# Selector and region products of layer one as 32x128 tiles instead of pairs of 32x64 tiles

## The reference, cut to what matters

```python
x = x + _L0_conv_ref(_gn(x), ...)      # shifted windows of 8x8 pixels, 16 heads of 16 channels
x = x + _L1_conv_ref(_gn(x), ...)      # causal and anti-causal attention over the whole image
```

```python
q = (xw @ Wq.T).reshape(-1, N, HEADS, d).transpose(0, 2, 1, 3)   # N = 64 tokens of a window, d = 16
k = (xw @ Wk.T).reshape(-1, N, HEADS, d).transpose(0, 2, 1, 3)
v = (xw @ Wv.T + bv).reshape(-1, N, HEADS, d).transpose(0, 2, 1, 3)
qn = q / jnp.maximum(jnp.linalg.norm(q, axis=-1, keepdims=True), 1e-12)
kn = k / jnp.maximum(jnp.linalg.norm(k, axis=-1, keepdims=True), 1e-12)
logits = jnp.einsum('bhnd,bhmd->bhnm', qn, kn) * scale
logits = logits + 16.0 * jax.nn.sigmoid(bias)
lg = jnp.where(mask[None, :, None], -jnp.inf, lg)                # mask: pixels of different regions
scores = jax.nn.softmax(logits, axis=-1)
o = jnp.einsum('bhnm,bhmd->bhnd', scores, v)
z = o @ Wo.T + bo
```

## Time and profile before

| | |
|---|---|
| median of 3 runs | 1212.93 us (1212.18 to 1214.43) |
| the profiled execution | 1214.44 us, its span 1212.7 us |
| TensorE busy | 1127.4 us, 93% |
| weight loads busy | 837.4 us, 69% |
| VectorE busy | 930.5 us, 77% |
| ScalarE busy | 640.7 us, 53% |
| one exponential of layer one (L621), mean | 1021 ns |
| mean granted TensorE clock | 0.969 of 2.4 GHz |

### The profile page before, as it was taken

The page is one execution under the profiler, slowest core; times in us unless marked ns, Lnnn a source line. Parts: engine busy times, 40 slices in busy tenths (PEclk is TensorE's granted clock), DMA queues, the critical chain, the costliest instruction groups (busy, mean ns, idle before and its releaser), DMA issues.

```text
span 1212.7 us, 50934 instructions
## 1 busy us (share of the span) xinstructions
PE 1127.4 (93%) x21342; PEld 837.4 (69%) x21342; DVE 930.5 (77%) x1669; ACT 640.7 (53%) x1051; POOL 199.9 (16%) x271
## 2 busy tenths in 40 slices
PE   6989998899799899979899999999999999999994
PEld 3767776777677677767667777777777777777762
DVE  4588888788788688864688788787878788787873
ACT  3465666566466456542545555555555555555550
POOL 1001111111011111111212221221222221221220
PEclk9799999899899899998999999999999999999997
DMA  2111111111111110000022222312222221312223
GB/s 85 49 37 40 42 42 29 39 37 38 40 37 37 41 38 23 24 23 11 10 55 46 63 54 51 70 39 67 44 62 44 61 56 49 70 40 65 44 65 78
DMA packets 189177, 55.93 MB, mean 46 GB/s; under 512 B 151172, under 2 KB 184214, under 8 KB 189078
## 3 DMA queue, kind: packets, MB, share of 16 engines
q1 hardware_dynamic: 184800, 53.06, 18.3%
q10 hardware_dynamic: 4280, 1.40, 0.5%
HBM read 35.95 MB, written 18.35 MB: 45 GB/s over the span
## 4 chain that ended last, share of the span: by engine, by line
PE 72%; DVE 15%; issue 7%; ACT 2%; DMA 2%; SPq 1%; DVEq 1%; ACTq 0%
PE psG L1103 13%; PE psA L500 10%; PE psA L1145 7%; PE psG L1125 5%; PE psE L1203 5%; PE psA L1164 5%; PE psA L1178 4%; PE psE L454 3%; DVE probs L736 3%; PE psA L488 3%; PE psA L440 3%; DVE stack L1430 3%; DVE stack L1425 3%; PE psE L475 2%; PE psG L396 2%
## 5 line engine op out<-in xcount | busy, mean ns | idle before, releaser
L1399 DVE TENSOR_REDUCE cm<-psG 128x4 f32<-128x1024 f32 (+1 forms) x192 | 234.9, 1224 | 117.0 <-PE psG L1125 116.9
L1261 ACT ACTIVATE probs<-psG 128x1024 f32<-128x1024 f32 x192 | 196.4, 1024 | 128.1 <-PE psG L1103 127.7
L1103 PE MATMUL psG<-stack 32*128 32x256 f32 (+1 forms) x2048 | 218.3, 341 | 7.1 <-DVE cm L1399 6.5
L1112 PE MATMUL psG<-stack 32*128 32x256 f32 (+1 forms) x2048 | 220.2, 342 | 1.7 <-DVE cm L1399 1.7
L1478 POOL TENSOR_SCALAR_AFFINE_SELECT probs<-probs 128x1024 f32<-128x1024 f32 x128 | 139.6, 1103 | 471.6 <-ACT probs L1261 471.5
L1103 PEld LDWEIGHTS psG<-stack 32*128 32x128 f32 x2048 | 149.8, 185 | 64.2 <-DVE cm L1399 27.6
L1112 PEld LDWEIGHTS psG<-stack 32*128 32x128 f32 x2048 | 149.9, 185 | 3.4 <-DVE cm L1399 1.9
L886 POOL TENSOR_TENSOR X<-X,probs 128x96 f32 (+5 forms) x128 | 55.0, 461 | 513.0 <-ACT probs L628 513.0
L500 PE MATMUL psA<-probs,xh 128*128 128x512 f32 x256 | 129.7, 633 | 2.1 <-ACT xh L661 1.4
L1164 PE MATMUL psA<-xh,wqk 128*128 128x256 f32 x512 | 121.5, 381 | 0.0
L1425 DVE RECIPROCAL stack<-stack 128x128 f32<-128x128 f32 x128 | 115.7, 929 | 4.0 <-DMA stack<-totals 4.0
(11 more groups left out here) (140 smaller groups left out, 1803.7 us busy)
## 6 DMA issues: line engine op xcount, KB each, us to landing
X<-in_xr SPq DMA_DIRECT2D x32, 256.0 KB, 3.7
probs<-inverses SPq DMA_DIRECT2D x32, 256.0 KB
stack<-scratch_heads SPq DMA_DIRECT2D x32, 256.0 KB
stack<-totals SPq DMA_DIRECT2D x64, 128.0 KB
out<-X SPq DMA_DIRECT2D x32, 256.0 KB, 3.0
scratch_heads<-stack SPq DMA_DIRECT2D x126, 64.0 KB
totals<-stack SPq DMA_DIRECT2D x126, 4.0 KB
inverses<-rd SPq DMA_DIRECT2D x32, 32.0 KB, 1.5
```

What stands on the lines that cost most here:

```text
L1103: last = nc.tensor.matmul(G[:, to:to + b.size], km[i.k][own_rows(r), o, e, b.keys_of(o) * P:(b.keys_of(o) + 1) * P], qm[i.k][own_rows(r), ...
L1112: nc.tensor.matmul(G[:, to:to + b.size], qm[j.k][own_rows(r), o, e, b.queries_of(o) * P:(b.queries_of(o) + 1) * P], km[j.k][own_rows(r), o ...
L1261: nc.scalar.activation(weights[i.k][:, b.weights_at:b.weights_at + 1024], G[:, base:base + 1024], ACT.Exp).then_inc(exp_done, 1)
L1399: nc.vector.reduce_max(slots, scores, AX_X).then_inc(max_done, 1)
```

## The change

In both places two products, one for each half of the output's partitions, become one product over all 128. The constants already lie side by side in SBUF (`pick` for e = 0 and 1, `region_queries` for the two windows), so no data moves. Each of the two stages now issues 8 products instead of 16 for an image, with the same 256 moving elements. The signals stay four for each stage. Everything else, the transpose of the maxima into the sums' bank included, is as it was.

```diff
@@ scores
                 for o in range(CT):
-                    for e in range(2):
-                        for r in range(QUADS):
-                            at = r * 512 + o * TOKENS
-                            last = nc.tensor.matmul(G[e * WTOK:(e + 1) * WTOK, at:at + TOKENS], pick[own_rows(r), 2 * o + e, :],
-                                                    ct[own_rows(r), :], start=False, stop=True,
-                                                    tile_position=(r * COL, e * WTOK), skip_group_check=True)
-                            if o == CT - 1 and e == 1:
-                                last.then_inc(s_ready, 1)
+                    for r in range(QUADS):
+                        at = r * 512 + o * TOKENS
+                        last = nc.tensor.matmul(G[:, at:at + TOKENS],
+                                                pick[own_rows(r), 2 * o:2 * o + 2, :].rearrange("p e k -> p (e k)"),
+                                                ct[own_rows(r), :], start=False, stop=True,
+                                                tile_position=(r * COL, 0), skip_group_check=True)
+                        if o == CT - 1:
+                            last.then_inc(s_ready, 1)
@@ bounds
                 for t in range(TT):
-                    for ww in range(2):
-                        for r in range(QUADS):
-                            at = r * 512 + t * TOKENS
-                            last = nc.tensor.matmul(G[ww * WTOK:(ww + 1) * WTOK, at:at + TOKENS],
-                                                    region_queries[own_rows(r), win(2 * t + ww)], region_keys[own_rows(r), :, :],
-                                                    start=False, stop=True, tile_position=(r * COL, ww * WTOK),
-                                                    skip_group_check=True)
-                            if t == TT - 1 and ww == 1:
-                                last.then_inc(max_ready, 1)
+                    for r in range(QUADS):
+                        at = r * 512 + t * TOKENS
+                        last = nc.tensor.matmul(G[:, at:at + TOKENS], region_queries[own_rows(r), t * P:(t + 1) * P],
+                                                region_keys[own_rows(r), :, :], start=False, stop=True,
+                                                tile_position=(r * COL, 0), skip_group_check=True)
+                        if t == TT - 1:
+                            last.then_inc(max_ready, 1)
```

## The result

| | before | after |
|---|---|---|
| median | 1213.12 us (1212.18 to 1214.43, 4 runs) | 1236.51 us (1233.68 to 1249.0, 4 runs) |
| ratio after to before | | 1.0212, 95% interval 1.0142 to 1.0282 |
| span of the profiled execution | 1212.7 us | 1233.7 us |
| TensorE busy, matmul records | 1127.4 us, 21342 | 1141.3 us, 20830 |

The change made the kernel slower by 23 us. The forecast, 4 us slower, had the sign and a sixth of the size, and the range ended at 1220.5.

What follows compares the result with a forecast made beforehand. VectorE was taken to pace 15 steps and a late TensorE 17, one of them hidden; 16 steps by 0.25 us gave 4.0 us, corrections cancelling, on 1212.93: 1216.9 us. Own range 1215 to 1219, wider range 1211.5 to 1220.5.

Steps and rivals of the forecast that it cites:

- The circle and the margin: VectorE's L736 to TensorE's L488, L500 and back takes 14.45 us; TensorE's margin before L488 is 0.69 or 0.30 us.
- The stop: Going from 32x64 to 32x128 tiles drains TensorE: 0.15 us before the selectors, 0.20 us before the region products.
- The slow load: Rival: 128 columns of a 32-row tile load slowly, 8.3 us more, 1221.2 us; chance 0.15 shared with a new issue wait.
- What hides it: The margin before L488 covers the added 0.25 us, so the 15 steps paced by VectorE cost nothing.
- The sum: Added TensorE time over 16 steps, 4.0 us; low clock, at most 0.75 more, and 0.9 less issue waiting cancel.
- the instructions arrive sooner: Rival: at L396 in three loop steps, shorter code removes issue waits, 7.8 us against the 4.0, 1209.1 us; chance 0.07.
- its converse: A new issue wait at a place like L396, 1219 to 1221 us; chance 0.15 shared with slowly loading weights.
- It must just happen to reach over that point: Condition for losing an issue wait at L396: a 4% instruction saving must reach the place where code is missing.
- The 16 steps by 0.25 us: Steps where TensorE is late, each paying 0.13 us at the selectors and 0.12 at the region products: 4.0 us.
- the hidden case: Rival: TensorE's added delay vanishes in later waits for issue, time near 1214 us; chance 0.20.
- the no-stop case: Rival: TensorE does not drain between 32x64 and 32x128 tiles, 1.9 us less, 1211.0 us; chance 0.08.

Runs made afterwards that it cites:

- the pair with equal code: Kernel before with 192 idle instructions at the start, 1203.49 us, and the same with 32x128 tiles and each product cut in two, 1204.58 us.
- the estimate above: Kernel before with 192 idle instructions at the start, less its 12.2 us of later start: would be at 1191 us, not run.

## Why the prediction was wrong

- *The circle and the margin*: right. The short rounds are 29.5 us before and after, and the margin shrank by the stops. In the pair with equal code the wait before the weighing went from 0.62 to 0.47 us and from 0.22 to none, where 0.37 and none were worked out.
- *The stop*: right, 0.15 and 0.20 us, the rounds 0.11 to 0.12 apart. From the last product of the stage ahead to the last one of the changed stage it is now 0.28 and 0.33 us in the raw starts (188.730 to 189.008 and 192.415 to 192.745), where 0.29 and 0.34 were worked out. The slow load did not come: it would have made them 0.39 and 0.44 us.
- *What hides it*: right for the steps in which VectorE sets the pace, as the equal short rounds show.
- *The sum*: this is the step that failed, "if the waits for issue, 15.3 + 8.3 = 23.6 us, shrink with them, 0.9 us is given back". I took the waits for issue to be a rate, so much waiting for so many instructions, and let them shrink by the 4% of instructions that go. Those of L396 in the loop come from rounds in which the loop is loaded again, each 6 to 7 us longer than a short one, and their number went from 3 to 7. The term was -0.9 us and measured +25.7 us in the loop. The trace of the kernel before already tells it, nine instruction packets in one round and none in the next; I had stayed with the waits.
- *The rivals*: "the instructions arrive sooner" named the place and had the wrong side; its converse, one new wait in some place, I priced at 2 to 4 us and not at four rounds. "It must just happen to reach over that point" was the right thought: either half of the change brings the loop to a place where it stays resident, and the whole change moves it on to one where it reaches further into an eighth block than before.
- *The 16 steps by 0.25 us*, 4.0 us: not confirmed. The pair with equal code shows 1.1 us between medians, inside the noise, and outside the loop the shorter code of the changed kernel is 4.7 us faster, not slower. What of that the stops took and what the code's new place gave was not told apart.
- *The chances* were added up with small slips, which do not bear on the outcome: the hidden case and half of the no-stop case are 0.24 and not 0.22, and what is left for faster is 0.11.

## What to carry to other kernels

Where TensorE's loop is about as long as here (1645 to 1709 instructions), look at the queue of instruction packets before anything else: rounds with packets and rounds without tell whether the loop stays resident. Then any edit that adds or takes instructions, in the loop or anywhere ahead of it, is also a move of the loop, and is to be measured at the same place in its blocks, or its own effect drowns in a much larger one. Here the same edit reads +2.1%, and -2% with 62 idle instructions ahead, while between kernels whose loop stays resident nothing of the edit can be seen: 1190.9 to 1194.2 us with one half or both, and about 1191 (the estimate above) without it.

## What the runs showed of the hardware that was not expected

- A TensorE loop of 1645 to 1709 instructions stays on the chip over ten rounds, or is loaded again in some of them in 9 packets of 16 KB, by its place alone. Such a round takes 5 to 8 us longer over all runs. How often it is loaded again goes with how far it reaches beyond its seventh block: 18 or 27 packets where it reaches 1 to 36 instructions into the eighth, 63 or 71 for 49 to 84, 90 for 73 to 108. What makes the choice from round to round was not found; that the block behind the loop is loaded meanwhile and pushes out its first would fit nine packets for eight blocks, and is only argued.
- The second loop, 1032 instructions, brought no packets between 740 and 1135 us in any run.
- An idle instruction costs TensorE 0.075 us, once there are more of them than the wait that they stand in hides; with 192 at the start, 12.2 us, they cost more than half of what the better place gives back.
